# A transformer in one program: when each stage takes up its first chunk, and how two feed-forwards prepare weights

## The reference

```python
x = x + _L0_attn_ref(_layernorm(x, axis=-1), ...)   # causal softmax attention, 16 heads of 8, power-law mask
x = x + _L0_ffn_ref(_layernorm(x, axis=-1), ...)    # silu(x Wg) * (x Wu), then Wd; integer weights * 1/127, 384 wide
x = x + _L1_attn_ref(...)                           # rotary attention over the batch pair
x = x + _L1_ffn_ref(...)                            # low-rank experts, two of six
x = x + _L2_attn_ref(...)                           # linear attention, running sums
x = x + _L2_ffn_ref(...)                            # 8 experts of width 256, gelu, a layernorm in each, two of eight weigh
x = x + _L3_attn_ref(...)                           # random-feature linear attention
x = x + _L3_ffn_ref(...)                            # 8 experts of width 512, tokens gathered by expert
```

## Time and profile before

| | us |
| --- | --- |
| median of 3 runs | 1120.84 |
| the 3 runs | 1120.64, 1120.84, 1128.33 |
| profiled execution, its own time | 1129.11 |
| its span | 1127.3 |
| outside the span | 1.8 |

### The profile page before, as it was taken

One profiled execution on the slowest core, in us unless ns is written; L12 is line 12 of the kernel. 1 busy time (PEld: TensorE's weight loads), 2 busy tenths in 40 slices (PEclk: granted clock), 3 DMA queues, 4 the chain that ended last, 5 costly groups with the idle time before them and its releaser, 6 DMA issues. The chain is left out here.

```text
span 1127.3 us, 17905 instructions
## 1 busy us (share of the span) xinstructions
PE 908.3 (81%) x6590; PEld 612.6 (54%) x6590; DVE 646.1 (57%) x1445; ACT 429.1 (38%) x1018; POOL 510.8 (45%) x458
## 2 busy tenths in 40 slices
PE   4558999999998878267899789995998996398983
PEld 2113333333433446154566678885895766388883
DVE  6757676767670155979687556778103666542324
ACT  2324664665556421014111365674344211032221
POOL 4335978897888611052322344554200001156561
PEclk9658999999998988758799599998899998599997
DMA  4800110011000000001000000121100000266664
GB/s 156 238 1 2 29 31 13 18 30 30 3 1 23 1 22 8 0 15 39 1 2 2 10 10 19 46 95 33 43 1 1 1 10 28 77 199 207 201 205 137
DMA packets 38747, 55.95 MB, mean 50 GB/s; under 512 B 6682, under 2 KB 26146, under 8 KB 38534
## 3 DMA queue, kind: packets, MB, share of 16 engines
q1 hardware_dynamic: 36166, 49.70, 14.9%
q0 software_dynamic: 2496, 5.12, 1.4%
HBM read 43.66 MB, written 10.94 MB: 48 GB/s over the span
## 5 line engine op out<-in xcount | busy, mean ns | idle before, releaser
L671 DVE TENSOR_REDUCE arena<-ps 128x2 f32<-128x1024 f32 (+2 forms) x192 | 177.6, 956 | 87.6 <-PE ps L487 55.4
L420 POOL TENSOR_TENSOR arena<-arena 128x1024 f32<-128x1024 f32 (+3 forms) x105 | 201.2, 1957 | 37.9 <-ACT arena L606 37.8
L606 ACT ACTIVATE arena<-ps 128x512 f32<-128x512 f32 (+3 forms) x320 | 138.6, 489 | 89.4 <-PE ps L519 56.2
L117 POOL TENSOR_SCALAR vareps<-meanvar 128x4 f32<-128x4 f32 x32 | 8.0, 251 | 236.2 <-DVE meanvar L98 236.2
L511 PE MATMUL ps<-arena 51*128 51x512 bf16 (+3 forms) x384 | 91.0, 342 | 18.1 <-ACT arena L606 6.8
L511 PEld LDWEIGHTS ps<-arena 51*128 51x128 bf16 x384 | 27.0, 94 | 105.0 <-ACT arena L606 58.6
L2076 PE MATMUL ps<-arena 128*128 128x128 f32 x624 | 78.2, 280 | 0.0
L152 PE MATMUL ps<-ident,xn 128*128 128x128 f32 x128 | 26.4, 356 | 62.1 <-DVE x L922 19.9
L2076 PEld LDWEIGHTS ps<-arena 128*128 128x128 f32 x624 | 74.7, 196 | 0.0
L420 POOL TENSOR_TENSOR xnT<-xnT,arena 128x1024 f32<-128x1024 f32 (+1 forms) x28 | 52.7, 1902 | 40.5 <-ACT xnT L606 40.5
L487 PE MATMUL ps<-arena 48*128 48x512 bf16 (+3 forms) x320 | 56.8, 351 | 16.8 <-DVE arena L671 14.1
(11 more groups left out here) (340 smaller groups left out, 2034.4 us busy)
## 6 DMA issues: line engine op xcount, KB each, us to landing
arena<-in_L_ffn_w SPq DMA_DIRECT2D x39, 512.0 KB
arena<-scratch SPq DMA_DIRECT2D x32, 192.0 KB, 4.0
arena<-in_L_ffn_w SPq DMA_DIRECT2D x16, 256.0 KB, 3.3
scratch<-arena SPq DMA_DIRECT2D x12, 256.0 KB, 4.0
arena<-expert_rows SPq DMA_DIRECT2D x8, 256.0 KB, 4.7
scratch<-arena SPq DMA_DIRECT2D x4, 384.0 KB, 5.7
scratch<-arena SPq DMA_DIRECT2D x12, 128.0 KB, 4.2
x<-in_x SPq DMA_DIRECT2D x4, 256.0 KB, 3.9
```

The costliest lines, as they stand in the source:

```text
L420: nc.gpsimd.tensor_tensor(e, e, weight[:, at:at + k].unsqueeze(1).broadcast_to([P, 2, k]), ALU.mult).then_inc(weighed, 1)
L606: nc.scalar.activation(probs(g)[:, 2 * p + e, 0:wd], m.ps[:, BANK[h, e], 0:wd], ACT.Exp, scale=SCALE).then_inc(exps, 1)
L671: nc.vector.tensor_reduce(out, scores, AX.X, ALU.max, negate=True).then_inc(max_set, 1)
```

## The change

Five things change.

1. **Roots by chunk.** A chunk's root becomes a function of its own (`root`). The attention and the feed-forward of layer 2 get it from the following stage and write it in the midst of their POOL queue: the attention after positions 9 and 13 (chunks 0 and 1), the feed-forward after steps 30 and 31. The other roots stand where they stood.
2. **Norm by chunk.** The attention of layer 2 is now `early`, so that the normalise of chunks 0 and 1 moves from behind the last statistics up behind the adds of chunks 1 and 2. The feed-forward of layer 2 stays `early=False`.
3. **Turns by chunk.** The wait of PE for the last chunk of x goes, at all eight stages. So that a turn cannot write a PSUM bank still in use, the attention of layer 2 turns in banks 5 and 6, its feed-forward in 7 and 3, and the gate product of the last stage goes to bank 0 instead of 5.
4. **Feed-forward of layer 0.** Gate and up products take float32r: w_up holds the integers themselves, which float32r holds exactly, and x goes as x_high and x_low, so each product is two float32r matmuls. The scale 1/127 goes into silu and, squared, into the down weights. ACT widens the integers in two instructions (`widen`), and DVE's L747 goes.
5. **Feed-forward of layer 2.** `round_weights`, `split_weights` and `sum_weights` for the next expert move from c = 1 to c = 0; on ACT and POOL they also move ahead of the step's squares and scales.

```diff
@@ Norm.gpsimd
-        for c in range(NC):
-            ts = slice(c * TPC, (c + 1) * TPC)
-            pool.wait_ge(m.ln_var, 2 * self.value(c))
-            nc.gpsimd.tensor_scalar(m.vareps[:, ts], m.meanvar[:, ts, 1], LN_EPS, None, ALU.add).then_inc(m.ln_rstd, 1)
-            pool.wait_ge(m.ln_rstd, 2 * self.value(c) - 1)
-            nc.gpsimd.tensor_tensor(m.rstd[:, ts], m.vareps[:, ts], m.power[:, ts], ALU.pow).then_inc(m.ln_rstd, 1)
+        while self.counted_roots < NC:
+            self.root(pool, self.counted_roots)
...
@@ wait_xnT
-        if self.turned == 0:
-            pe.wait_ge(*self.before.ready[NC - 1])
-            if self.k == 0:
-                pe.wait_ge(m.set_up, 2)
-                pe.wait_ge(m.consts_in, 16 * (2 + len(BIASES)))
+        if self.turned == 0 and self.k == 0:
+            pe.wait_ge(m.set_up, 2)
+            pe.wait_ge(m.consts_in, 16 * (2 + len(BIASES)))
@@ l0_ffn
+    m.rounded.fresh()
+    x_high, x_low = norm.split_xnT()
+    w_up = m.rounded.take("l0f_w_up", [P, 2, F], F32R)
...
-    def dequantise(dve):
-        dve.wait_ge(w_in, w_all)
-        nc.vector.tensor_scalar(w[:, :, :], wi[:, :, :], SCALE, None, ALU.mult).then_inc(w_scaled, 1)
+    def widen(act):
+        act.wait_ge(w_in, w_all)
+        nc.scalar.activation(w_up[:, :, :], wi[:, 0:2, :], ACT.Copy).then_inc(w_set, 1)
+        nc.scalar.activation(w_down[:, :], wi[:, 2, :], ACT.Copy, scale=SCALE * SCALE).then_inc(w_set, 1)
...
-                    nc.tensor.matmul(m.ps[:, 2 * (s % 2) + half, :], w[:, half, f * P:(f + 1) * P], m.xnT[:, c * CH:(c + 1) * CH],
-                                     start=True, stop=True).then_inc(up_done, 1)
+                    out, lhsT = m.ps[:, 2 * (s % 2) + half, :], w_up[:, half, f * P:(f + 1) * P]
+                    nc.tensor.matmul(out, lhsT, x_high[:, cs], start=True, stop=False)
+                    nc.tensor.matmul(out, lhsT, x_low[:, cs], start=False, stop=True).then_inc(up_done, 1)
...
-            nc.scalar.activation(sg[:, s % 2, :], m.ps[:, 2 * (s % 2), :], ACT.Silu).then_inc(sg_done, 1)
+            nc.scalar.activation(sg[:, s % 2, :], m.ps[:, 2 * (s % 2), :], ACT.Silu, scale=SCALE).then_inc(sg_done, 1)
@@ l2_attn
+    norm.banks = (5, 6)
...
+            if t >= 2 * TPC and t % TPC == 1:
+                root(pool, t // TPC - 2)
...
-                before_norm={"gpsimd": clear}, bias="L2_attn_bo", early=False)
+                before_norm={"gpsimd": clear}, bias="L2_attn_bo", roots=True)
@@ l2_ffn
+    norm.banks = (7, 3)
...
+            if c == 0 and e + 1 < E:
+                round_weights(e + 1)
             if n:
                 squares(n - 1)
-            if c == 1 and e + 1 < E:
-                round_weights(e + 1)
...
+            if c == 0 and e + 1 < E:
+                split_weights(e + 1)
             if n >= 4:
                 pool.wait_ge(y_set, n - 3)
             pool.wait_ge(squared, n + 1)
...
-            if c == 1 and e + 1 < E:
-                split_weights(e + 1)
+            if n > STEPS - NC + 1:
+                root(pool, n - (STEPS - NC + 2))
...
-            if c == 1 and e + 1 < E:
+            if c == 0 and e + 1 < E:
                 sum_weights(e + 1)
...
-                early=False)
+                early=False, roots=True)
```

More of the change, by code:

```diff
@@ L32, in __init__ @@
     def __init__(self, ready, tensor=None, vector=None, scalar=None, gpsimd=None, sync=None,
[L33 to L34 removed]
+                 before_norm=None, bias=None, early=True, roots=False):
+        self.ready, self.before_norm, self.bias, self.early, self.roots = ready, before_norm or {}, bias, early, roots
         self.tensor, self.vector, self.scalar, self.gpsimd, self.sync = tensor, vector, scalar, gpsimd, sync
@@ L127, in gpsimd, with root @@
                 self.add_bias(pool, bias, c)
+    def root(self, pool, c):
+        nc, m = self.nc, self.m
+        assert c == self.counted_roots
+        self.counted_roots += 1
+        ts = slice(c * TPC, (c + 1) * TPC)
+        pool.wait_ge(m.ln_var, 2 * self.value(c))
+        nc.gpsimd.tensor_scalar(m.vareps[:, ts], m.meanvar[:, ts, 1], LN_EPS, None, ALU.add).then_inc(m.ln_rstd, 1)
+        pool.wait_ge(m.ln_rstd, 2 * self.value(c) - 1)
+        nc.gpsimd.tensor_tensor(m.rstd[:, ts], m.vareps[:, ts], m.power[:, ts], ALU.pow).then_inc(m.ln_rstd, 1)
     def add_bias(self, pool, bias, c):
@@ L1470, in scalar, with gpsimd @@
             if n == 4:
-                for c in range(NC):
-                    turn(c)
+                for k in range(NC):
+                    turn(k)
+            if c == 0 and e + 1 < E:
+                round_weights(e + 1)
             if n:
                 squares(n - 1)
-            if c == 1 and e + 1 < E:
-                round_weights(e + 1)
         squares(STEPS - 1)
-    def gpsimd(pool):
+    def gpsimd(pool, root):
         def split_weights(e):
@@ L2043, in tensor @@
                 norm.wait_xnT(pe, t // TPC)
-            last = nc.tensor.matmul(m.ps[:, 5, t * E:(t + 1) * E], m.xnT[:, t * P:(t + 1) * P], gate[:, :], start=True, stop=True)
+            last = nc.tensor.matmul(m.ps[:, 0, t * E:(t + 1) * E], m.xnT[:, t * P:(t + 1) * P], gate[:, :], start=True, stop=True)
         last.then_inc(logits.sem, 1)
@@ L2425, in program, with root @@
         following = {id(a): b for (a, _), (b, _) in zip(built, built[1:])}
+        def root(norm):
+            return following[id(norm)].root if id(norm) in following else lambda pool, c: None
         def after(norm):
@@ L2485, in _ @@
                 norm.gpsimd(pool, m.bias_of.get(part.bias))
-                if part.gpsimd:
+                if part.gpsimd and part.roots:
+                    part.gpsimd(pool, root(norm))
+                elif part.gpsimd:
                     part.gpsimd(pool)
```

20 lines of the change are left out of this document (10 added, 10 removed).

## The result

| | before | changed |
|---|---|---|
| median of 20 runs each, same chips | 1127.28 us | 1111.92 us |
| lowest to highest | 1120.00 to 1131.74 us | 1105.03 to 1124.36 us |
| profiled execution (span) | 1129.11 us (1127.3) | 1110.74 us (1108.9) |

The ratio is 0.987, with a 95% interval of 0.9849 to 0.9891: 14.7 us less, between 12.3 and 17.0. (Ratios leave out executions counted as slow, two of the changed kernel's 20 and one of e6's four, at 3838.89 us, so 14.7 stands here and not the 15.4 between the medians.) 1102.1 was forecast, with a range of 1094 to 1112. The time lies at the very end of the range. The direction was right, the size was not.

The account below looks back on a forecast made before the run. No single bound: PE, busy 81% of the span, loses time to float32 matmuls, waits for prepared weights and gaps between stages. Terms 7.8 + 10.1 + 0.3 + 0.5 = 18.7 us off the 1120.84 median give 1102.1, range 1094 to 1112.

Parts of the forecast that it names:

- The base: Whole kernel: the 18.7 us saving was taken off the earlier median of 1120.84 us, not the profiled 1129.11.
- The weights: Feed-forward 2: preparing expert weights a step earlier removes six PE waits on POOL's w1_low and slower restarts, minus 10.1 us.
- Feed-forward 0: Layer 0's feed-forward: float32r gates and ups, with an earlier start, bring its last add 7.8 us sooner.
- Attention 2 into feed-forward 2: Normalises moved into attention 2's loop cost 1.9 us, earlier turns and x_low start feed-forward 2 sooner: minus 0.3 us.
- its start: Start of attention 2: turns come earlier by up to 2.2 us, but DVE is the next late, minus 0.5 us.
- The other starts: Starts of feed-forward 1, attention 3, attention 1, first and last stage: something as late remains, 0 each, up to minus 0.8.
- (a): Rival, feed-forward 0: POOL's x_low and DVE's normalises obstruct each other, 5.2 us back, 1107.3 us; chance 0.13.
- (b): Rival, feed-forward 2: DVE's late mean delays POOL's scales, about 1 us in each of seven experts, 1109 us; chance 0.10.
- (c): Rival, feed-forward 0: PE pauses for DVE and runs at half clock, 48 us instead of 28, 1122 us; chance 0.06.
- (d): Rival, feed-forward 2: half clock makes steps 6.8 us instead of 3.40; nine of 32 give 1133 us; chance 0.04.
- (e): Rival, stage starts: x_low behind all roots and paired turns eat the early turns, moved normalises cost 2 us, 1105; chance 0.06.
- the prediction's signs: New profile: feed-forward 0's last add 7 to 8 us earlier, experts 13.6 us, w1_low wait gone, attention 2 2 us longer.

Follow-up runs that it names:

- e6: Changed kernel with ACT's two copies of the next chunk in feed-forward 0 behind the chunk's first silu; ratio to before 0.9849, feed-forward 0 32.6 us.
- e1: Kernel before, with only feed-forward 2's weight preparation one step earlier; ratio 0.9939, 6.9 us less, feed-forward 2 149.3 us instead of 159.4.
- e10: Changed kernel with the weights of feed-forward 2's last expert alone prepared where they were before; ratio to before 0.9808, attention 3 159.2 us.
- e12: Changed kernel with copies behind the first silu in feed-forward 0 and feed-forward 2 early too; ratio to before 0.9803, median 1106.60 us.
- e3: Changed kernel with feed-forward 0 and feed-forward 2's weight preparation put back, leaving early turns, roots in loops and attention 2's moved normalises; ratio to before 1.0008.
- e5: Changed kernel with PE's wait for the last x back ahead of attention 2's first turn only; ratio to before 0.9888, attention 2 114.6 us.
- e11: Changed kernel with copies behind the first silu, feed-forward 2 early and attention 2's normalises back at its end; ratio to before 0.9818, median 1105.63 us.
- e8: Changed kernel run again unaltered, to see what repeats; ratio to before 0.9868, six stages 532.5 us.
- e9: Kernel before with the changed feed-forward 0 and feed-forward 2 weight preparation, no early turns, roots in loops or moved normalises; ratio 0.9802, median 1106.41 us.

## Why the prediction was off, point by point

**The base: the step that failed first.** "... so the same 18.7 comes off the median: 1102.1". That median was of three runs, 7.7 us apart; of twenty it is 1127.28, 6.4 higher. The profiled execution, 1129.11, was the better witness. From 1127.28 the same sum gives 1108.6, and then 3.3 us are missing. For the profiled execution the prediction has 1110.4, and 1110.74 was measured; that is luck. Of the 18.4 us between the two profiles only 13.6 lie in the six stages, and 4.8 in the last stage, for which the sum has nothing.

**The sum: 18.7 was said, 13.6 (12.2 in the repeat) is in the six stages, 14.7 in the times.** The 5.1 between 18.7 and 13.6 are 1.4 in feed-forward 0, 3.3 in attention 2 and feed-forward 2 together (10.9 was said, 7.6 measured) and 1.7 in attention 3, which the sum puts at nothing, less 1.3 won in attention 1 and feed-forward 1. Term by term:

- *The weights, 10.1.* Right as a mechanism and to the digit in its own stage (e1: 10.1). "I take the full value, since every engine beside PE has 4 us free" looked at the other engines only. 1.7 to 1.9 of it came back in attention 3, as clock, and e10 shows that this hangs on the last of the gaps.
- *Feed-forward 0, 7.8.* A size: 6.4, 5.6 in the repeat. "x_high costs four more copies on ACT, 0.65 each, hidden by ACT's idle 26 us" is the sentence that failed. Idle time of the stage isn't idle time at that place in the queue: down products without a normalise between them came 6.94 apart where 6.5 was said, with a normalise 7.59 where 7.6 was. The copies' place costs 1.2 us (e6 against e10). The rest is how long half level lasts in the first and the last chunk, which moves this stage by 2.8 us in one and the same code (e6, e12); e6's 8.3 has the better of it.
- *Attention 2 into feed-forward 2, 0.3, and its start, 0.5.* Said were 1.9 more in the loop against 2.2 in feed-forward 2's start and 0.5 in attention 2's. 2.2 is what e3 shows. The loop's cost is 2.9 to 3.1 at the same clock (e5 against before, e12 against e11), so 1.9 was under-sized by 1.0 to 1.2. The 0.5 was there too: the first scores came 8.2 us earlier, after a last add 7.6 earlier. The clock, for which the sum has no term, took 0.9 to 1.8 us on top (against e5), and gave 2.6 on e12's path.
- *The other starts, 0.* Right: the first turn of attention 3 waits 12.16 where it waited 12.26, and DVE's normalise holds feed-forward 1. The 1.1 that feed-forward 1 gained did not repeat (0.3 in e8) and is not shown to be an effect of the change.

**The rivals.** (a) *POOL and DVE*: it did happen, at feed-forward 0's first chunk (a normalise of 3.02 us at 401.64) and in feed-forward 2's start (3.01). By the Trainium skill, "SBUF — State Buffer", section "Who interferes with whom", the port pair that the two share is an exclusive lock. The trace agrees: 3.01 and 3.02 against 1.3. But in feed-forward 0 PE's first product waited for POOL and not for that normalise, and no later normalise of feed-forward 0 met an x_low (1.08 us each, at 424.13 and 431.72), so its 5.2 us did not come. (b) *The wait on POOL moves*: no, PE is busy for 13.60 of 13.60 us. (c) and (d) *Half clock*: the right mechanism, priced as a whole stage or nothing and put in the two stages where gaps closed. It came in pieces of 1 to 2 us, in attention 2, attention 3 and the first and last chunk of feed-forward 0. The argument against (d), "it held 1.00 with them", was true of feed-forward 2 and said nothing of the stages behind it. (e) *It doesn't begin with the first chunk*: nearest to the truth for the title's part, which is worth nothing (e3, e9).

**The chances.** Faster by over 1% had 0.85 and came, with 1.3%, though 1111.92 is not below the 1109.6 that was named for it, since the base moved. The forecast's own band, 1097 to 1108, missed. The widest unknown, the base, was named ("part of a case may land higher") but got no share of the range. The range's upper end, "9 us less", isn't the sum of the terms' own ends either: together these give about 1 us less (2.6 and 0 less, 2 more, 0.5 less). Of the prediction's signs, experts of 13.6 us, the vanished wait for w1_low and float32r matmuls about 0.24 apart came. The last add of feed-forward 0 came 5.6 us sooner behind its first product (29.7 and not 35.4), where 7 to 8 was said, and attention 2 grew by 4.7, where 2 was.

**Open.** The last stage is 4.8 us shorter in the profile after than in that before, and in all profiles 177.7 to 188.6. The four without the title's part have 177.7 to 188.6, the ten with it 178.8 to 185.7, so nothing shows that any of it belongs to the change. Why a pause at 741 us sets the clock at 913 was not tried.

## What to carry to other kernels

A gap that is closed on TensorE pays at once in its own stage, but later stages can give part of it back through the clock, so a change's worth is read from the stage lengths of two or more profiles and not from the stage that was edited. An extra copy on an engine with idle time costs something if it stands in the queue ahead of the instruction that the next wait hangs on; look at the place, not at the share. And take the base of a forecast from the run that the trace is of, or widen the range by the spread of the few runs that are shown.

## What the runs showed of the hardware

The same stage with the same instructions ran at a different granted clock depending on what TensorE did long before: 0.60 or 0.70, 0.72 or 0.83, and 0.85 or 0.95 in three windows of 8 us, for one pause of 1.3 us some 35 us and some 170 us earlier (e10; the lower values in all seven profiles without the pause in which the stage starts in the same way). Identical code also took one of two paths by chance of the execution, 34.1 and 116.4 us or 34.9 and 115.5 in feed-forward 1 and attention 2, and a third, 34.0 and 112.0, in e12, which differs in other stages only. And one wait of 1.87 us was followed by full level in one profile and by half level in another (48 matmuls in 5.52 or 6.77 us). So with waits of this size the level is not a property of the wait.
